# Two-part fp32r scores in head pairs, with own opening and ending, in an attention and channel-mix block

## The chip, the cores and the metric

The kernel runs on one core of a Trainium2 chip. The metric is device time in microseconds of one execution, the median of the runs. The core's engines work side by side, each through its own program in order: TensorE (PE; its weight loads are shown as PEld), VectorE (DVE), ScalarE (ACT), GpSimd (POOL), and SyncE (SP), which here only issues transfers. They meet at semaphores.

## What is computed

Eight sequences (B = 8) of N = 1024 tokens with D = 256 channels go through an adaptive layer norm, causal attention with 16 heads of 16 channels, a gated residual, a second adaptive norm and a channel mix with a token shift, gated into the residual again. The reference, cut to what matters:

```python
mod = (silu(c) @ wmod).reshape(8, 6, 1, -1)
sa, ca, ga, sb, cb, gb = (mod[:, i] for i in range(6))
ga, gb = (sign(g) * maximum(abs(g), 0.25) for g in (ga, gb))
h = layernorm(x) * (1 + ca) + sa
q, k, v = split(h @ w_in.T)                 # 16 heads of 16
p = softmax(where(causal, -inf, q @ k.T * 16 ** -0.5))
x = x + ga * ((p @ v) @ w_out.T + b_out)
h = layernorm(x) * (1 + cb) + sb
prev = h shifted by one token, zero first
xr, xk = mu_r * h + (1 - mu_r) * prev, mu_k * h + (1 - mu_k) * prev
x = x + gb * sigmoid(xr @ W_r.T) * (square(relu(xk @ W_k.T)) @ W_v.T)
```

Everything is float32. Products are made from parts: a value is rounded to a high part, what is left is a low part, and products of parts are added up.

## The kernel before

**Tiles.** A batch is one sequence. Its 16 heads are taken in G = 4 head groups (s = 0 to 3) of four heads, and each group in STEPS = 12 steps (t). Step t of COL_STEPS takes 128 keys against a stretch of 128, 256, 384 or 512 queries: keys 0 to 511 against the first half of the queries (t = 0 to 3), then keys 0 to 1023 against the second (t = 4 to 11). Six steps are 512 wide, and two each are 384, 256 and 128; 4608 query columns per head in all.

**Scores.** `fill_stacks` builds, for every head group, operands of 96 rows: six products of bf16 parts of q and k (Q_PARTS, K_PARTS), 16 rows each, placed by 12 transfers for either half of the tokens. Scores are computed twice. `row_unit` (L1052) makes them with queries on the partitions, 128 queries against a stretch of keys, into one of three banks `row_ps`; on the diagonal it adds a causal mask by a further product (L1081). VectorE reduces each bank to a maximum (`maximum`, L871). `split_max` cuts the maxima into three bf16 parts, TensorE turns them (L1066), and SyncE puts them as three more rows into the next stack. `score_columns` (L1035, L1046) makes the scores again with keys on the partitions, the maxima already subtracted, into one of three banks `col_ps`. ScalarE takes the exponential (`exps`, L715) into `weights`, GpSimd clears the part above the diagonal (L597), and `values` (L1100) multiplies with v and a column of ones, four heads side by side in four column tiles of 32, in float32. The maxima of group s + 1 are made while group s goes through exponentials.

**Dense work.** Everything else on TensorE shares the one bank `dense_ps`: the next batch's front (`front_unit`: four transposes of normalised rows at s = 1, four projections to q and k at s = 0 and s = 2 each, four to v at s = 0) and the last batch's back (`back_unit`: five units "out", "norm", "recept", "key", "value" for each quarter of the tokens, at steps BACK_STEPS after the quarter's start). TensorE takes the bank when the one before has been emptied (`claim_dense`). Around these lie the elementwise chains on the other engines: statistics and normalising on VectorE (L900, L910), the reciprocal root on GpSimd, rounding to high parts on ScalarE, low parts on GpSimd (L609, L611, L617, L638, L659, L663), gating and residuals on VectorE and GpSimd (L968, L971, L636, L671, L673).

**Order.** Each engine's program is written out by `pipeline` and `timeline`: a "first" batch with front work only, "start", "second", five "mid" and "last", then a "drain" in which the last batch's back work is done alone, its quarters TAIL_LAG = 5 ticks apart. PER_STEP says how many maxima units a step holds, and TensorE spreads them between its other instructions. Before the first batch the weights are rounded into two parts in one piece (L693 on ScalarE, L824 on VectorE), and `gates` (L840 to L854) prepares the output gates. `reciprocals` (L949) inverts the softmax sums, which go through memory and come back spread over the partitions, and L960 applies them to the attention output (`att_n`).

## Time and profile before

| | us |
|---|---|
| median of 3 runs | 1707.06 (1705.77 to 1711.83) |
| the profiled execution, its own time | 1706.89 |
| its span, first to last instruction | 1705.1 |
| TensorE busy in the span | 1407.6 |
| VectorE busy | 1184.0 |
| ScalarE busy | 911.2 |
| GpSimd busy | 738.6 |

The profile is of one execution. Busy time is the union of an engine's instructions. The ends of matmuls are modelled, so their starts are the safer reading: the distance from one start to the next is what an instruction costs when nothing is waited for. A wait is named by the engine and tile that wait and the instruction that ended it.

### The profile page before, as it was taken

To read this page: it belongs to the slowest core of one execution; us is meant where nothing else is said; L and a number is where in the kernel's file an instruction comes from. 1 tells how busy PE (TensorE), PEld (TensorE's weight loads), DVE (VectorE), ACT (ScalarE), POOL (GpSimd) and SP (SyncE) were. 2 spreads that over 40 slices of the span, in tenths; PEclk is the share of its full clock that TensorE was granted. 3 is DMA by queue.
4 is the path that set the end of the run, shared out by engine and by line. 5 is a ranking of instruction groups with operands and counts; after the bars stand their busy time and mean duration, and the time that the engine had idled before them with its cause. 6 is when DMAs were issued, how large, how long until landed. Compare 5 with 4: busy or idle time off the path is not lost.

```text
span 1705.1 us, 28546 instructions
## 1 busy us (share of the span) xinstructions
PE 1407.6 (83%) x9913; PEld 743.8 (44%) x10024; DVE 1184.0 (69%) x2306; ACT 911.2 (53%) x1795; POOL 738.6 (43%) x878
## 2 busy tenths in 40 slices
PE   3698989788887888788897888879888888989754
PEld 2253444344543445444443445434454444444344
DVE  4767667877677776877678676777767777777232
ACT  2056555555556555555555555565655655566521
POOL 4223223444454543545344444535435543444555
PEclk9899999999999999999999999989999999999956
DMA  3211121111321122111311113211221112111200
GB/s 105 63 62 52 49 94 59 49 46 57 101 68 39 46 73 93 43 55 48 102 53 50 39 58 102 67 35 48 68 95 51 57 43 80 47 61 42 65 25 19
DMA packets 101840, 102.61 MB, mean 60 GB/s; under 512 B 21296, under 2 KB 89912, under 8 KB 101696
## 3 DMA queue, kind: packets, MB, share of 16 engines
q1 hardware_dynamic: 98176, 91.59, 16.5%
q0 software_dynamic: 2560, 8.39, 1.3%
q8 instruction: 80, 1.31, 0.3%
q10 hardware_dynamic: 960, 0.79, 0.2%
q14 instruction: 64, 0.52, 0.1%
HBM read 31.74 MB, written 8.94 MB: 24 GB/s over the span
## 4 chain that ended last, share of the span: by engine, by line
PE 49%; DVE 22%; ACT 9%; POOL 7%; issue 7%; SPq 3%; DMA 2%; another core or an unknown queue 1%; POOLq 0%; DVEq 0%; ACTq 0%
PE row_ps L1076 9%; PE col_ps L1046 9%; PE val_ps L1100 8%; DVE max_a L871 8%; PE dense_ps L1110 7%; PE dense_ps L1112 5%; PE dense_ps L1111 5%; ACT weights L715 4%; PE row_ps L1081 2%; SPq L459 2%; DVE xn_c L910 2%; DVE mixed L984 2%; PE dense_ps L1129 1%; DVE max_b L871 1%
## 5 line engine op out<-in xcount | busy, mean ns | idle before, releaser
L715 ACT ACTIVATE weights<-col_ps 128x512 f32<-128x512 f32 (+1 forms) x1216 | 621.7, 580 | 461.1 <-PE col_ps L1046 342.2
L871 DVE TENSOR_REDUCE max_a<-row_ps 128x1 f32<-128x512 f32 (+3 forms) x864 | 550.0, 663 | 229.2 <-PE row_ps L1081 143.8
L1076 PE MATMUL row_ps<-k_stack,q_stack 125*128 125x512 bf16 (+3 forms) x1536 | 460.6, 338 | 58.7 <-DVE max_a L871 36.1
L1046 PE MATMUL col_ps<-q_stack,k_stack 128*128 128x512 bf16 (+3 forms) x1425 | 362.5, 328 | 52.4 <-ACT weights L715 39.9
L597 POOL TENSOR_SCALAR_AFFINE_SELECT weights<-weights 128x512 f32<-128x512 f32 x256 | 169.7, 663 | 526.2 <-ACT weights L715 520.7
L1100 PE MATMUL val_ps<-weights,v_ones 128*32 128x512 f32 (+3 forms) x3072 | 331.7, 504 | 18.1 <-POOL weights L597 16.5
L1076 PEld LDWEIGHTS row_ps<-k_stack,q_stack 125*128 125x128 bf16 x1536 | 144.7, 98 | 354.4 <-DVE max_a L871 173.3
L871 DVE TENSOR_REDUCE max_b<-row_ps 128x1 f32<-128x384 f32 (+3 forms) x352 | 213.0, 635 | 107.1 <-PE row_ps L1081 106.7
L1046 PEld LDWEIGHTS col_ps<-q_stack,k_stack 128*128 128x128 bf16 x1536 | 132.3, 98 | 202.7 <-ACT weights L715 130.8
L1081 PE MATMUL row_ps<-causal,ident_bf 128*128 128x128 bf16 x1024 | 203.1, 223 | 0.0
L1100 PEld LDWEIGHTS val_ps<-weights,v_ones 128*32 128x32 f32 x3072 | 60.9, 108 | 112.3 <-issue 66.0
L1081 PEld LDWEIGHTS row_ps<-causal,ident_bf 128*128 128x128 bf16 x1024 | 102.5, 100 | 14.6
L984 DVE SCALAR_TENSOR_TENSOR mixed<-h_diff,mus,h 128x256 f32<-128x256 f32 x128 | 76.3, 655 | 20.5 <-POOL h_diff L652 20.4
L659 POOL TENSOR_TENSOR mix_lo<-mixed,mix_hi 128x512 fp32r<-128x512 f32 x64 | 81.3, 1292 | 6.8 <-ACT mix_hi L782 6.8
L652 POOL TENSOR_TENSOR h_diff<-h 128x512 f32<-128x512 f32 x32 | 33.3, 1041 | 93.0 <-ACT h L774 92.3
L1110 PE MATMUL dense_ps<-h_hi,w_hi 128*128 128x512 f32 x128 | 61.3, 479 | 7.9 <-DVE qk_rest L942 4.2
L1129 PE MATMUL dense_ps<-ident,xn_c 128*128 128x128 f32 x128 | 21.8, 296 | 52.0 <-DVE xn_c L910 50.0
L1110 PE MATMUL dense_ps<-w_hi,o_hi 128*128 128x256 f32 x128 | 40.6, 317 | 25.2 <-POOL o_lo L638 18.9
L723 ACT ACTIVATE val_out<-val_ps 128x512 f32<-128x512 f32 x64 | 38.8, 606 | 29.0 <-PE val_ps L1100 28.5
L1110 PE MATMUL dense_ps<-mix_hi,w_hi 128*128 128x256 f32 x128 | 40.4, 316 | 15.1 <-ACT h_hi L758 12.1
L736 ACT ACTIVATE v_ones<-dense_ps 128x512 f32<-128x512 f32 x32 | 20.1, 628 | 61.0 <-PE dense_ps L1112 61.0
L1112 PE MATMUL dense_ps<-h_hi,w_lo 128*128 128x512 f32 x128 | 51.5, 403 | 0.0
(128 smaller groups left out, 2254.3 us busy)
## 6 DMA issues: line engine op xcount, KB each, us to landing
q_stack<-q_part SPq DMA_DIRECT2D x384, 64.0 KB, 2.5
k_stack<-k_part SPq DMA_DIRECT2D x372, 64.0 KB, 2.5
xa<-in_x SPq DMA_DIRECT2D x8, 1024.0 KB, 7.5
att<-val_out SPq DMA_DIRECT2D x64, 128.0 KB
recips<-recip_rows SPq DMA_DIRECT2D x32, 256.0 KB
xq<-in_x SPq DMA_DIRECT2D x28, 256.0 KB, 2.9
out<-xq POOLq DMA_DIRECT2D x28, 256.0 KB, 2.6
q_stack<-max_rows SPq DMA_DIRECT2D x192, 4.0 KB
```

The lines of the kernel that those rows point to most:

```text
L597: nc.gpsimd.affine_select(out=w, in_=w, compare_op=ALU.is_ge, fill=0.0, base=0, pattern=[[0, G], [1, P]], channel_multiplier=-1).then_inc( ...
L659: nc.gpsimd.tensor_tensor(mix_lo[:, m], mixed[:, m], mix_hi[:, m].bitcast(F32), ALU.subtract).then_inc(mix_lo_done, 1)
L715: nc.scalar.activation(weights[:, t % 2, h:h + n, 0:q1 - q0], col_ps[bank][:, 0:n * (q1 - q0)].rearrange("p (h q) -> p h q", h=n), ACT.Exp ...
L871: nc.vector.reduce_max(dest, bank[:, 0:len(heads) * (k1 - k0)].rearrange("p (h k) -> p h k", h=len(heads)), AX_X).then_inc(max_done, 1)
L984: last = nc.vector.scalar_tensor_tensor(mixed[:, m, c, :], h2_diff[:, c, :], mus[:, m, c:c + 1], h2[s % 2][:, c, 0:QT], ALU.mult, ALU.add)
L1046: last = nc.tensor.matmul(col_ps[bank][:, i * (q1 - q0):(i + 1) * (q1 - q0)], k_stack[s % 2][:, h, P * j:P * (j + 1)], q_stack[s % 2][:, h ...
L1076: last = nc.tensor.matmul(bank[:, n * width:(n + 1) * width], q_stack[stack][0:MAX_AT, h, P * i:P * (i + 1)], k_stack[stack][0:MAX_AT, h, ...
L1081: last = nc.tensor.matmul(bank[:, (n + 1) * width - P:(n + 1) * width], ident_bf[:], causal[:], start=False, stop=end, skip_group_check=True)
L1100: last = nc.tensor.matmul(val_ps[32 * h:32 * h + 32, q0 - base:q1 - base], v_ones[:, j, G * s + h].rearrange("p d a -> p (d a)"), weights[ ...
L1110: nc.tensor.matmul(dst, a_hi(c), b_hi(c), start=(c == 0), stop=False)
L1111: nc.tensor.matmul(dst, a_hi(c), b_lo(c), start=False, stop=False)
L1112: last = nc.tensor.matmul(dst, a_lo(c), b_hi(c), start=False, stop=(c == KC - 1))
```

## The change

Scores are made from two fp32r parts instead of three bf16 ones, so three products of 16 rows and two rows of maxima, 64 rows per head. Two heads, one in rows 0 to 63 and one in rows 64 to 127, are issued one behind the other into different banks. Banks are two for columns and four for rows. The maxima are gathered as columns of one tile, cut in two parts by two reductions, and turned by one transpose of 128 by 128. Maxima units come in two groups a step, at its start and after the values or the second score pair. Normalising moves from VectorE to ScalarE as scale and shift, between the exponentials; GpSimd makes the shift. The full-precision h moves from ScalarE to VectorE. The attention gate is multiplied into the output weights once per batch on GpSimd, in place of a product per quarter. Two of the four projections to v move to the batch before (s = 3), and the back units lie one step later. The opening has a program of its own on every engine, which puts the four row tiles through four banks, rounds the weights in two pieces and makes the first projections; the ending starts the last batch's quarters at ticks TAIL_START, from step 8 of the last head group, each with a bank of its own, with three elementwise steps moved from GpSimd to VectorE and the residual read from `xa`. The diff, cut to its core:

```diff
+COL_BANKS, ROW_BANKS = 2, 4
...
-Q_PARTS = (0, 0, 0, 1, 1, 2)
-K_PARTS = (0, 1, 2, 0, 1, 0)
+Q_PARTS = (0, 0, 1)
+K_PARTS = (0, 1, 0)
 ROWS = len(Q_PARTS) * HD
-MROWS = 3
-MAX_AT = P - MROWS
-FILL = 2 * len(Q_PARTS) * 16
+MROWS = 2
+ROW_TILE = 64
+MAX_AT = ROW_TILE - MROWS
+FILL = 2 * 2 * len(Q_PARTS) * 16
+PLACED = 2 * MROWS * 16
+MAX_COLS = (32, 48, 64)
 
 
...
+def bank_heads(width):
+
+    return ((0, 2), (1, 3)) if width <= QT else ((0,), (1,), (2,), (3,))
+
+
+COL_HEADS = [bank_heads(q1 - q0) for q0, q1, _ in COL_STEPS]
...
-PER_STEP = [2, 3, 3, 3, 3, 4, 4, 5, 5, 4, 2, 1]
...
+PER_STEP = [4, 4, 4, 4, 5, 2, 4, 4, 2, 4, 2, 2]
...
-V_STEPS, QK_STEPS, T_STEPS = (0, 1, 2, 3), (4, 6, 7, 8), (4, 6, 8, 10)
+V_EARLY, V_STEPS, QK_STEPS, T_STEPS = (7, 9), (0, 3), (4, 5, 7, 8), (3, 5, 7, 9)
...
-BACK_STEPS = dict(zip(BACK_UNITS, (2, 5, 9, 10, 13)))
...
+BACK_STEPS = dict(zip(BACK_UNITS, (2, 6, 10, 11, 13)))
+BACK_END = 16
+
+TAIL_START = (8, 11, 15, 18)
+TAIL_TICKS = TAIL_START[-1] + BACK_END - STEPS
...
+            def place_max(stack, half):
+
+                for part in range(MROWS):
+                    for odd in range(2):
+                        row, lo = ROW_TILE * odd + MAX_AT + part, 8 * (2 * part + odd)
+                        sp.dma_start(stack[row:row + 1, half].rearrange("p g n -> p (g n)").bitcast(F32),
+                                     max_rows[half][lo:lo + 8, :].bitcast(F32)).then_inc(max_placed[half], 16)
...
+            def gate_out_weights(b):
+
+                pool.wait_ge(gates_att_in, (b + 1) * 16)
+                pool.wait_ge(ready["transposed"], b * 4 + (8 if b < B - 1 else 4))
+                wait(pool, w_out_done, b)
+                g = gates_att[:, 0:1, :].broadcast_to([P, KC, D])
+                nc.gpsimd.tensor_tensor(gated[:], w_out[:], g, ALU.mult).then_inc(w_gated, 1)
+                pool.wait_ge(w_gated, b + 1)
+                wait(pool, ready["out"], b * G)
+                hi, lo = (w[:, W_O:W_ALL].rearrange("p (k n) -> p k n", k=KC) for w in (w_hi, w_lo))
+                nc.gpsimd.tensor_copy(hi, gated[:]).then_inc(w_out_hi_done, 1)
+                pool.wait_ge(w_out_hi_done, b + 1)
+                nc.gpsimd.tensor_tensor(lo, gated[:], hi.bitcast(F32), ALU.subtract).then_inc(w_out_done, 1)
 
...
+            def normalise(src, rstd, shift, dst, shift_done, done, count):
+
+                act.wait_ge(shift_done, count)
+                for i in range(2):
+                    last = nc.scalar.activation(dst[:, i, :], src[:, i, :], ACT.Identity, bias=shift[:, i:i + 1],
+                                                scale=rstd[:, i:i + 1])
+                last.then_inc(done, 1)
...
+            def normalise_next(b, kind, s, t):
+
+                if s == 1 and fronts(kind) and attends(kind) and t in T_STEPS:
+                    k = T_STEPS.index(t)
+                    count = b * 4 + (4 + k + 1)
+                    wait(act, ready["transposed"], count - 1)
+                    normalise(xa[:, 2 * k:2 * k + 2, :], rstd_a, shift_a, xn_a, shift_a_done, xn_a_done, count)
...
+                whole = parts[:, MAX_COLS[0]:MAX_COLS[0] + 16].bitcast(F32)
                 if half:
-                    nc.vector.tensor_tensor(src, src, max_b[:], ALU.max).then_inc(max_chain, 1)
+                    spans = parts[:, MAX_COLS[1]:MAX_COLS[1] + 32].bitcast(F32)
+                    nc.vector.reduce_max(whole, spans.rearrange("p (n c) -> p c n", n=2), AX_X).then_inc(max_chain, 1)
                     chain = chain + 1
                     dve.wait_ge(max_chain, chain)
-                nc.vector.tensor_scalar(parts[:, :, 0:G], src, -1.0, None, ALU.mult).then_inc(max_chain, 1)
...
+                pairs = parts[:, 0:64].bitcast(F32).rearrange("p (n c) -> p c n", n=2)[:, 0:16, :]
+                with nc.allow_low_precision("each output is one part of two, rounded as a part"):
+                    nc.vector.tensor_reduce(parts[:, 0:16], whole.rearrange("p (c n) -> p c n", n=1), AX_X, ALU.max,
+                                            negate=True).then_inc(max_chain, 1)
+                    dve.wait_ge(max_chain, chain + 1)
+                    nc.vector.tensor_reduce(parts[:, 16:32], pairs, AX_X, ALU.add, negate=True).then_inc(max_split, 1)
...
+            def rest_of_front(b, kind, s, t):
+
+                unit = front_unit(b, kind, s, t - 1)
+                if unit and unit[0] == "transposed":
+                    _, k, count = unit
+                    mod = mod_t[:, 8 * (b + 1):8 * (b + 1) + 4]
+                    dve.wait_ge(h_hi_done, count)
+                    wait(dve, h_lo_done, count - 1)
+                    for c in range(KC):
+                        last = nc.vector.tensor_scalar(h_full[:, c, :], dense_ps[:, c, :], mod[:, 2 + c:3 + c],
+                                                       mod[:, c:c + 1], ALU.mult, ALU.add)
+                    last.then_inc(free["transposed"], 1)
                 if unit and unit[0] == "qk":
...
+                if tail and u == 2:
+
+                    dve.wait_ge(o_hi_done, q + 1)
+                    nc.vector.tensor_tensor(o_lo[:], att_n[:, :, QT * s:QT * (s + 1)], o_hi[:].bitcast(F32),
+                                            ALU.subtract).then_inc(o_lo_done, 1)
+                if tail and u == 13:
+
+                    dve.wait_ge(k_hi_done, q + 1)
+                    nc.vector.tensor_tensor(k_lo[:], k_sq[:], k_hi[:].bitcast(F32), ALU.subtract).then_inc(k_lo_done, 1)
+                if tail and u == 15:
+
+                    dve.wait_ge(scaled_done, q + 1)
+                    nc.vector.tensor_tensor(xr, xr, recept_of(b, s), ALU.add).then_inc(out_done, 1)
+                if u == 4:
...
+                pair = COL_HEADS[t][c - COL_FIRST[t]:c - COL_FIRST[t] + 2]
+                for i in range(len(pair[0])):
+                    for odd, heads in enumerate(pair):
+                        bank, ago = bank_of(COLS * s + c + odd, COLS * G, COL_BANKS)
+                        if i == 0:
+                            wait(pe, exp_done, exp_index(b, s, c + odd) + (1 - ago))
+                        rows = slice(ROW_TILE * odd, ROW_TILE * (odd + 1))
+                        last = nc.tensor.matmul(col_ps[bank][:, i * (q1 - q0):(i + 1) * (q1 - q0)],
+                                                stack_at(k_stack[s % 2], rows, heads[i], P * j, P * (j + 1)),
+                                                stack_at(q_stack[s % 2], rows, heads[i], q0, q1),
+                                                start=(i == 0), stop=(i == len(heads) - 1), skip_group_check=True)
+                        if i == len(heads) - 1:
+                            last.then_inc(cols_ready, 1)
+
...
+                for n in range(len(pair[0])):
+                    for odd, heads in enumerate(pair):
+                        if n == 0:
+                            banks[odd] = row_bank(b, s, u + odd)
+                        rows = slice(ROW_TILE * odd, ROW_TILE * odd + MAX_AT)
+                        end = n == len(heads) - 1 and not diagonal
+                        last = nc.tensor.matmul(banks[odd][:, n * width:(n + 1) * width],
+                                                stack_at(q_stack[stack], rows, heads[n], P * i, P * (i + 1)),
+                                                stack_at(k_stack[stack], rows, heads[n], k0, k1),
+                                                start=(n == 0), stop=end, skip_group_check=True)
+                        if end:
+                            last.then_inc(rows_ready, 1)
+                for n in range(len(pair[0])) if diagonal else ():
+                    for a in range(2):
+                        for odd in range(2):
+                            rows = slice(ROW_TILE * odd, ROW_TILE * (odd + 1))
+                            end = n == len(pair[0]) - 1 and a == 1
+                            last = nc.tensor.matmul(banks[odd][:, (n + 1) * width - P + ROW_TILE * a:(n + 1) * width],
+                                                    mask_ident[rows, a, :], mask_fill[rows, a, ROW_TILE * a:P],
+                                                    start=False, stop=end, skip_group_check=True)
+                            if end:
+                                last.then_inc(rows_ready, 1)
 
             def values(b, s, t):
...
+            def open_first():
+
+                pe.wait_ge(consts_done, 3)
+                for k in range(4):
+                    pe.wait_ge(xn_a_done, k + 1)
+                    transposes(row_ps[k][:].rearrange("p (c n) -> p c n", c=KC), xn_first[:, 2 * k:2 * k + 2, :]
+                               ).then_inc(ready["transposed"], 1)
+                gate_sums()
+                pe.wait_ge(w_qk_done, 1)
+                for k in range(4):
+                    pe.wait_ge(h_lo_done, 2 * (k // 2 + 1))
+                    wait(pe, free["qk"], k - 1)
+                    qk_unit(qk_banks[k % 2], 0, k).then_inc(ready["qk"], 1)
+                pe.wait_ge(w_done, 1)
+                pe.wait_ge(setup_done, 1)
+                for k in range(2):
+                    v_unit(v_banks[k], k).then_inc(ready["v"], 1)
+                pe.wait_ge(free["v"], 2)
 
             def front(unit):
...
+                dense = dense_of(b, s)
+                if b == B:
+
+                    if name == "out":
+                        pe.wait_ge(max_done, unit_index(B - 1, G - 2, MT1) + 1)
+                    else:
+                        before = BACK_UNITS[BACK_UNITS.index(name) - 1]
+                        pe.wait_ge(free[before], count)
...
+                    row_scores(b, s, early)
+                    for c in cols[:1]:
                         score_columns(b, s, t, c)
+                    if attends(kind) if t else has_late(kind, s):
+                        values(*last)
+                    dense_step = unit or any(back_unit(*item) for item in at)
+                    if dense_step:
+                        row_scores(b, s, late)
+                    for c in cols[1:]:
+                        score_columns(b, s, t, c)
+                    if not dense_step:
+                        row_scores(b, s, late)
                     if unit:
                         claim_dense()
                         front(unit)
+                    for item in at:
+                        if back_unit(*item):
+                            if item[0] < B:
+                                claim_dense()
+                            back(*item)
+                    if t == STEPS - 1 and has_rows(kind, s):
+                        turn_max(b, s, MT1)
+
...
```

## Rows read from the trace of the kernel before

**Rows 1.** The page: busy us (share of the span), instructions.

```profile
PE 1407.6 (83%) x9913; PEld 743.8 (44%) x10024; DVE 1184.0 (69%) x2306; ACT 911.2 (53%) x1795; POOL 738.6 (43%) x878
```

**Rows 2.** Stretches: us, busy us (instructions) by engine, clock, DMA share, GB/s.

```profile
59.70:84.40 24.70, 19.41 (x85) 7.31 (x87) 24.49 (x48) 0.01 (x1) 0.69 (x1) 0.76 0.32 65
...
90.40:247.90 157.50, 142.76 (x1027) 64.92 (x1040) 113.40 (x229) 95.41 (x189) 42.96 (x60) 0.97 0.15 51
...
641.60:843.20 201.60, 171.38 (x1239) 90.51 (x1251) 149.21 (x286) 113.03 (x225) 90.87 (x108) 0.98 0.19 62
...
1443.70:1614.00 170.30, 148.52 (x1085) 76.00 (x1096) 104.79 (x206) 99.73 (x198) 76.76 (x89) 0.99 0.18 56
1614.00:1705.10 91.10, 44.54 (x210) 38.97 (x208) 28.48 (x55) 19.83 (x35) 48.33 (x49) 0.63 0.06 23
```

**Rows 3.** Waits, 641.6 to 1443.7 us: us in total, times, longest us.

```profile
ACT weights L715 <- PE col_ps L1046: 181.6, 77, 5.9
PEld row_ps L1076 <- DVE max_a L871: 83.8, 115, 2.0
PEld col_ps L1046 <- ACT weights L715: 65.5, 122, 1.7
...
PE dense_ps L1129 <- DVE xn_c L910: 29.0, 16, 3.0
```

**Rows 4.** Timeline, TensorE, around 49.6 and 800 us: start us, us, instruction.

```profile
49.56 0.40 PE L1110 MATMUL dense_ps<-h_hi,w_hi 128*128 128x512 f32 x1
...
49.80 0.40 PE L1111 MATMUL dense_ps<-h_lo,w_hi 128*128 128x512 f32 x1
...
800.13 0.34 PE L1046 MATMUL col_ps<-q_stack,k_stack 128*128 128x384 bf16 x1
800.40 1.06 PE L1100 MATMUL val_ps<-weights,v_ones 128*32 128x512 f32 x8
801.40 0.34 PE L1076 MATMUL row_ps<-k_stack,q_stack 125*128 125x384 bf16 x1
...
801.92 0.28 PE L1112 MATMUL dense_ps<-w_hi,k_lo 128*128 128x256 f32 x1
802.04 0.28 PE L1110 MATMUL dense_ps<-w_hi,k_hi 128*128 128x256 f32 x1
...
803.27 0.22 PE L1081 MATMUL row_ps<-causal,ident_bf 128*128 128x128 bf16 x1
803.33 0.60 PE L1046 MATMUL col_ps<-q_stack,k_stack 128*128 128x256 bf16 x4
```

**Rows 5.** Groups by shape: times, busy us, mean ns, idle us before.

```profile
L1046 PEld LDWEIGHTS col_ps<-q_stack,k_stack 128*128 128x128 bf16 x1536 | 132.3, 98 | 202.7 <-ACT weights L715 130.8 <-issue 18.2
...
L1110 PEld LDWEIGHTS dense_ps<-w_hi,mix_hi 128*128 128x128 f32 x128 | 25.8, 201 | 15.2 <-issue 8.8 <-DVE mix_out L992 5.0 <-DVE gated L968 1.4
```

**Rows 6.** Timeline, merged: eleven VectorE maxima, six ScalarE exponentials in a row.

```profile
62.49 6.12 DVE L871 TENSOR_REDUCE max_a<-row_ps 128x4 f32<-128x512 f32 x11
...
1593.46 3.05 ACT L715 ACTIVATE weights<-col_ps 128x512 f32<-128x512 f32 x6
```

**Rows 7.** Timeline of the opening: ScalarE, then TensorE.

```profile
15.14 3.19 ACT L693 ACTIVATE w_hi<-v_ones 128x3584 fp32r<-128x3584 f32 x1 [7.32 <-DMA v_ones<-in_w_v_t]
...
59.68 0.29 PE L1076 MATMUL row_ps<-k_stack,q_stack 125*128 125x128 bf16 x1 [6.18 <-DMA k_stack<-k_part]
```

**Rows 8.** Timeline of the ending: TensorE, VectorE, GpSimd.

```profile
1609.99 0.43 PE L1100 MATMUL val_ps<-weights,v_ones 128*32 128x128 f32 x8 [2.34 <-POOL weights L597]
...
1619.30 0.52 DVE L949 RECIPROCAL sums<-sums 128x64 f32<-128x64 f32 x1
...
1626.80 1.67 DVE L960 TENSOR_TENSOR att_n<-att,recips 128x1024 f32<-128x1024 f32 x1 [5.33 <-DMA recips<-recip_rows]
...
1665.06 0.55 PE L1110 MATMUL dense_ps<-w_hi,o_hi 128*128 128x256 f32 x1 [5.38 <-POOL o_lo L638]
...
1701.01 0.75 POOL L675 DMA_DIRECT2D out<-weights  x1 [0.30 <-POOL weights L673]
```

798 lines of the change are left out of this document (422 added, 376 removed).

## The prediction

> **What bounds the kernel now.** I read the page first, for the engines' shares [rows 1], then cut the span into its stretches [rows 2], and then asked, for the middle stretches, who waits for whom [rows 3]. No engine is full: TensorE is busy 83% of the span, VectorE 69%, ScalarE 53%. The reader is to see three parts of the span [rows 2]. The opening lasts until the first value product at 90.4 us. Then come eight batches: 157.5 us for the first, which has no back work beside it, (1443.7 - 247.9) / 6 = 199.3 us on average for each of the six that follow (the row of 201.6 is one of them), and 170.3 for the last. The ending is 91.1 us with nothing left to overlap.
>
> Inside a batch TensorE is busy 171 of 201.6 us, but those ends are modelled, so I count starts. One head group (a quarter of a batch, twelve steps) streams 4 x 4608 = 18432 columns of scores for the exponentials and as many for the maxima. Starts lie 0.11 us apart at 256 columns [rows 4] (four of them in 0.60, less about 0.27 for the last one's own time), which is one column a cycle at 2.4 GHz: 7.7 us each. The 32 mask products at 0.06 (803.27 to 803.33) make 1.9. Values take 1.00 us at 512 columns from their first start to the next instruction, against 0.85 for the columns (four passes of 512) [rows 4]; over twelve steps 10.7. Dense work of a batch is 8 x 6 x 0.23 (512 columns) + 20 x 12 x 0.12 (256) [rows 4] + 8 x 0.45 for the norms' transposes (estimated at four loads of 0.11 each) = 43 us, so 10.7 per group. With 0.9 for turning the maxima this is 39.6 per group, 158 us per batch of 199.3. The other 41 us are waits. They are spread: for ScalarE to empty a column bank, for VectorE to empty a row bank, and for the second norm's transposes, 29.0 us in 16 waits over four batches, so 7 us per batch [rows 3]. ScalarE waits for TensorE, 181.6 us in the same 802 us, so it is not the bound. TensorE in program order, fed in turn by three buffers a side, sets the step.
>
> **The change on TensorE, per head group.** Scores become three products of 16 rows plus two rows of maxima, in 64 rows, so two heads stand in the array at a time, in tiles of 64 rows.
> - Columns for exponentials and for maxima: half the stream if the two tiles run together, -3.8 and -3.8. The trace has no row tile. The nearest rows are the value products, four column tiles whose eight instructions end 1.06 us after the first starts [rows 4], where one after another the columns alone would need 3.4; so tiles can overlap here. The bounds are -3.8 and 0 each; I take -3.8, because these rows show four tiles at full overlap.
> - Operands go from bf16 to fp32r. Its matmuls keep one column a cycle: 0.12 us at 256 columns [rows 4]. Its weight load reads 201 ns against 98 [rows 5], but comes every 0.12 us under the dense products. If the two tiles' loads queue, a pair costs two such pitches, about 0.22 us, whatever its width: 48 pairs, 10.6 us for both kinds against the 7.7 taken. Bounds 0 to +2.9; I take 0 for widths of 512 and leave the rest in the range.
> - Mask: 32 pairs of half-height products for 32 whole ones: 0.3 less. Maxima turned as two fp32r tiles for eight bf16 transposes: 0.3 less.
> - Every change of tiling costs: the value product starts 0.27 us after a 384-column score whose columns take 0.16, and leaves 0.05 to 0.15 behind it [rows 4]; 0.1 a change. Score to value and back is there already. New is the change between scores and dense work, in 36 of 48 steps, twice, and twice for each turning of maxima: 22 changes per group, +2.2. No row shows such a change with row tiles: bounds 0 to +4.4, and I take the middle, as the value product is the nearest row.
>
> Sum: -7.6 - 0.6 + 2.2 = -6.0 us per group, -24 per batch. TensorE's own 158 becomes 134.
>
> The Trainium skill speaks against this edit at one point. "TensorE: Matmul & The Clock Gate", section on fast weight load, says that the fast load is not given to FP32 inputs and that a load takes its columns at 1.2 GHz, 107 ns for 128. The trace agrees in the ratio (98 against 201 ns [rows 5]). By that page alone with loads queued the sum would be -3.1 instead of -6.0; with its statement in Part 3 that loads overlap other row groups it stays -6.0.
>
> **The other engines, per batch.** VectorE, 149 busy now [rows 2]: normalising goes (16 operations of 256 columns, estimated at no more than the 0.6 of a maximum [rows 6] each: -9); gating of the attention output is folded into the weights (four 512-wide operations, estimated at the 0.6 of a maximum each: -2.5); of nine short operations on the maxima per group four go, each followed by a wait for its own end (estimated -6); the full-precision h moves here from ScalarE (8 x 0.4 = +3.3). Two short units more add 0.3 a group (+1). About 136. ScalarE, 113 [rows 2]: 16 operations of 256 columns come and 8 go, none over the 0.5 of an exponential: 117. GpSimd, 91 [rows 2]: two operations per projection go, small shift operations and three on the gated weights come; it stays far from a bound. No queue becomes the bound: SyncE issues 12 stack transfers per half as before and 4 rows of maxima for 3, and it starts key stacks one wait earlier, which takes away the few waits for them.
>
> **From work to batch.** If the waits of 41 us stay, a batch is 199.3 - 24 = 175. Norm now has a step more after its statistics and the wait for its transposes should go, -7. Against it stand the column banks, two where there were three: the second pair of a step can only be streamed when exponentials of the first pair are done. A pair of 512-wide heads keeps ScalarE some 1.0 us (six exponentials in 3.05 [rows 6]), and TensorE has values or rows to put between. I count half a microsecond for every third of 20 pairs per group, 3.3 per group at most, and take +7 per batch of a bound 0 to +13. So 175, of a range 160 to 190.
>
> **The ends.** Opening: now the weights' rounding (3.19 us for all) waits until 15.1, four row tiles pass one after another through statistics, GpSimd, transposes, ScalarE and back, and the first score starts at 59.7 after projections, parts and transfers; VectorE is busy with the gates until 62.5 [rows 6], and 24.7 us of maxima follow [rows 2, 7]. After the change statistics and turns are pipelined through four banks, projections use two, the gates are taken between parts. I estimate the first score at 36, bounds 32 to 45, and leave the 24.7 us, which VectorE's 40 reductions at 0.56 set [rows 6]. First value product at 66 (62 to 75), against 90.4. Ending: the last value product starts at 1610.0; the reciprocals come only at 1619.3, at the fifth tick of VectorE's program, and reach att_n at 1626.8; then quarters wait for each other, since all share one dense bank and GpSimd: the last one's first product starts at 1665.1 [rows 8]. After the change half the quarters start in the last twelve steps, each quarter has a bank of its own, the reciprocals go three ticks earlier (-5), and three GpSimd operations a quarter move to VectorE or before. What stays is one chain: 12 us to the normalised values, 27 for a quarter's five products with splits between (1665.1 to 1701 is 36, with the sharing), 6 for the quarter behind it, 3 to store: 50 (44 to 62), against 91.1.
>
> **Sum.** 66 + first batch 133 (157.5 - 24, no norm to gain) + 6 x 175 + last batch 149 (170.3 - 24 + 3 for tail work) + 50 = 1448; with 1.8 us around the span (1706.89 - 1705.1) 1450. The profiled run is 0.2 us below the median of 1707.06, so nothing is to be corrected.
>
> **Rivals.**
> 1. Loads of the two tiles queue (+11.5 per batch), or the two column banks cost their bound: 1450 + 8 x 11.5 = 1542. For it: fp32r loads of 201 ns. Against it: the value products' eight loads, which don't hold back their 1.06 us.
> 2. The change does not do what it says: row tiles run one after another. The score gain of 7.6 per group is gone, 30 per batch: 1450 + 8 x 30 = 1690, of which all that is left is the two ends. The trace shows only column tiles, so it can't exclude this.
> 3. Slower: TensorE stands at the second column bank. Both tiles of a pair are issued in order, and the odd head's bank is freed one exponential (0.48 us, from 3.05 for six) after the even one's. If TensorE arrives early each time, it loses that for each of 20 pairs: 9.6 per group, 38 per batch, 1450 + 8 x 38 = 1754. The ends give 65 us, so it turns into a loss from (1707 - 1450) / 8 = 32 us per batch, that is 0.4 us at every pair. Against it: ScalarE waits for TensorE now rather than the reverse, and values, rows and dense work lie between pairs.
> 4. Better: the 41 us of waits shrink with the work, and the transposes' wait goes: 160 per batch, 1450 - 8 x 13 = 1346.
>
> **How the numbers follow.** My forecast (1400 to 1500) has 0.47, rival 1 (1500 to 1580) 0.21, rival 4 (below 1400) 0.15, rival 2 (1580 to 1700) 0.11, rival 3 0.06. The range of 8 in 10 is 1360 to 1580: it takes in the forecast, rival 1 and most of rival 4, and leaves out rivals 2 and 3 and what lies below 1360. A run of this kernel can tell about 0.5%, 8.5 us. Faster by more than that: 0.47 + 0.21 + 0.15, and 0.07 of rival 2, is 0.90; the same, out of rivals 2 and 3, 0.04; slower 0.06.
>
> **What would show it.** The score pairs' second matmul starting within 0.02 us of the first, and a 512-wide pair passing in 0.22 us, shows the main term; 0.43 shows rival 2. Pairs of 128 columns at 0.22 apart show queued loads. Waits of TensorE's score products for ScalarE of some 0.5 us, twenty per group, show rival 3. A batch should last 175 us, VectorE be busy some 136 of it, the first value product start near 66 and the last one end 50 before the end. What would make the prediction wrong is above all the waits: 41 us of 199 that I let stand because no row says how two banks and fuller reordering share them. The granted clock, 0.97 to 0.99 in the batches (2.4 GHz) [rows 2], must stay there with TensorE less busy; it was 0.63 in the ending, where TensorE was busy half the time.

## The result, and the profile after

The changed kernel takes 1581.45 us (median of 4 runs, 1577.35 to 1588.32), the kernel before 1706.41 beside it: a ratio of 0.9267 (0.9227 to 0.9307), faster by 7.3%. The forecast was 1450 us, faster by 15%; the time lies just above its range of 1360 to 1580. The profiled execution of the changed kernel took 1580.16 us with a span of 1578.3.

The page's busy line of the changed kernel answers [rows 1]:

```profile
PE 1389.9 (88%) x10856; PEld 798.2 (51%) x10856; DVE 1058.8 (67%) x2155; ACT 961.5 (61%) x1916; POOL 661.9 (42%) x874
```

VectorE is shorter by 125 us, ScalarE longer by 50, as meant. TensorE, whose scores were to take half their time, is busy for only 18 us less. The stretches of the changed kernel, cut at the first value product of each batch, answer [rows 2]. Columns: stretch, its length, busy us of PE, PEld, DVE, ACT, POOL, granted clock, DMA share, GB/s.

```profile
36.00:76.20 40.20, 30.50 (x166) 19.36 (x166) 28.16 (x58) 4.44 (x9) 0.65 (x1) 0.54 0.35 64
76.20:239.40 163.20, 149.61 (x1148) 74.32 (x1146) 110.94 (x223) 98.94 (x197) 34.88 (x55) 0.91 0.22 56
...
602.80:786.60 183.80, 167.06 (x1358) 95.44 (x1358) 128.61 (x265) 119.74 (x241) 83.81 (x112) 0.96 0.26 68
...
1332.90:1507.90 175.00, 157.54 (x1132) 83.62 (x1130) 94.96 (x191) 105.15 (x211) 74.80 (x92) 0.87 0.18 48
1507.90:1578.30 70.40, 35.80 (x217) 33.32 (x216) 24.63 (x49) 25.44 (x47) 34.08 (x42) 0.76 0.09 31
```

| stretch, us | before | forecast | after | forecast missed by |
|---|---|---|---|---|
| to the first value product | 90.4 | 66 | 76.2 | +10 |
| first batch | 157.5 | 133 | 163.2 | +30 |
| six middle batches | 199.3 each | 175 each | 182.3 each | +44 |
| last batch | 170.3 | 149 | 175.0 | +26 |
| ending | 91.1 | 50 | 70.4 | +20 |

All of the gain is in the middle batches (102 us) and the two ends (35 us); the first and the last batch are longer than before. The clock is the first thing to see: before, it was 0.97 to 0.99 in all eight batches [rows 2], now it is 0.91 in the first and 0.87 in the last. Cut into pieces of 5 us, most of the loss in the last batch lies in its last head group: pieces between 1475 and 1500 us stand at 0.50, which is 1.2 GHz, with TensorE's records covering 82 to 91% of them. Before it fell, TensorE had waited 2.40 us for GpSimd's clearing (0.16 us busy in 1472 to 1474); it is back at 1.00, 2.4 GHz, from 1504, behind 5.00 us busy in 1500 to 1505. There the last batch has no maxima to make and hardly any dense work; before, the same place held 1.00 until 1608.

The waits of the middle stretch (421.4 to 1332.9 us, five batches) answer [rows 3]. Columns: who waits for whom, us in total, times, longest. The last row, set apart, is of the kernel before (641.6 to 1443.7 us, four batches).

```profile
ACT weights L804 <- PE col_ps L1219: 195.2, 249, 3.5
DVE max_parts L1026 <- PE row_ps L1267: 189.2, 164, 3.2
PEld row_ps L1256 <- DVE max_parts L1026: 98.0, 157, 1.1
...
PEld col_ps L1219 <- ACT weights L804: 68.8, 127, 1.7
...
PEld val_ps L1288 <- POOL weights L656: 42.4, 70, 1.5
...
PE dense_ps L1317 <- ACT xn_c L848: 8.3, 15, 0.6
```

```profile
PEld val_ps L1100 <- POOL weights L597: 12.6, 15, 2.3
```

ScalarE and VectorE both wait for TensorE, and TensorE for both in many pieces of half a microsecond. Its wait for the second norm has gone, from 7 to 1.7 us a batch [rows 3]; its weight loads wait 14 us a batch for column banks (16 before) and 20 for row banks (25 before: the 83.8 us of [rows 3] and 16.7 for `max_b`, over four batches). One wait has grown: the loads for the values stand 8.5 us a batch for GpSimd's clearing of the part above the diagonal, where it was 3.2. These sums can overlap with waits of the matmuls themselves, so they are not added up.

TensorE's timeline around 802 us answers [rows 4]:

```profile
802.22 0.40 PE L1300 MATMUL dense_ps<-h_hi,w_lo 128*128 128x512 f32 x1
802.55 0.50 PE L1256 MATMUL row_ps<-k_stack,q_stack 62*128 62x512 f32 x2
802.88 0.40 PE L1219 MATMUL col_ps<-q_stack,k_stack 64*128 64x512 f32 x2
803.22 1.06 PE L1288 MATMUL val_ps<-weights,v_ones 128*32 128x512 f32 x8
804.21 0.73 PE L1219 MATMUL col_ps<-q_stack,k_stack 64*128 64x512 f32 x2
804.88 0.50 PE L1298 MATMUL dense_ps<-h_hi,w_hi 128*128 128x512 f32 x1
```

Two heads of 512 columns pass as one pair, so the row tiles do run together: rival 2 is out. But a pair whose columns take 0.213 us holds TensorE for 0.33 (802.55 to 802.88, 802.88 to 803.22). In the median a 512-wide pair takes 0.34 to another pair, 0.41 to values and 0.43 to dense work; before, a 512-wide bf16 product ahead of values took 0.31 to 0.32. The dense product ahead of a pair takes 0.33 where it takes 0.23 ahead of another dense one. These pitches are where the stream's gain went, and the first runs were made to price them.

### The profile page after: what moved, and what is told of

Read it like the earlier page. It is cut to its first block, busy times and chain, and to the rows that moved or that the text cites. A ratio compares the mean times of both kernels' runs of the same rounds, so it can differ in the third digit from the quotient of the medians.

```text
span 1578.3 us, 30222 instructions
## 1 busy us (share of the span) xinstructions
PE 1389.9 (88%) x10856; PEld 798.2 (51%) x10856; DVE 1058.8 (67%) x2155; ACT 961.5 (61%) x1916; POOL 661.9 (42%) x874
## 4 chain that ended last, share of the span: by engine, by line
PE 52%; POOL 12%; DVE 12%; issue 7%; SPq 7%; ACT 6%; DMA 4%; ACTq 0%; POOLq 0%; DVEq 0%
PE val_ps L1288 13%; PE col_ps L1219 11%; PE row_ps L1256 8%; PE dense_ps L1298 6%; SPq L494 6%; DVE max_parts L1026 6%; PE dense_ps L1299 4%; PE dense_ps L1300 4%; ACT weights L804 4%; POOL weights L656 3%; DMA xq<-in_x 2%; PE row_ps L1267 2%; POOL mix_out L733 2%; POOL xq L736 2%; DVE mixed L1120 1%
## 5 line engine op out<-in xcount | busy, mean ns | idle before, releaser
L1026 DVE TENSOR_REDUCE max_parts<-row_ps 128x1 f32<-128x512 f32 (+3 forms) x1280 | 748.9, 630 | 387.1 <-PE row_ps L1267 296.4
L804 ACT ACTIVATE weights<-col_ps 128x512 f32<-128x512 f32 (+2 forms) x1280 | 643.5, 556 | 373.0 <-PE col_ps L1219 366.5
L1219 PE MATMUL col_ps<-q_stack,k_stack 64*128 64x512 f32 (+3 forms) x1536 | 388.8, 424 | 16.3 <-ACT weights L804 14.7
L1256 PE MATMUL row_ps<-k_stack,q_stack 62*128 62x512 f32 (+3 forms) x1536 | 349.5, 431 | 27.8 <-DVE max_parts L1026 18.5
L1219 PEld LDWEIGHTS col_ps<-q_stack,k_stack 64*128 64x128 f32 x1536 | 197.4, 194 | 173.4 <-ACT weights L804 135.6
L1256 PEld LDWEIGHTS row_ps<-k_stack,q_stack 62*128 62x128 f32 x1536 | 167.8, 194 | 230.4 <-DVE max_parts L1026 150.8
L1267 PE MATMUL row_ps<-mask_fill,mask_ident 64*128 64x128 bf16 (+1 forms) x2048 | 134.2, 213 | 0.0
L1267 PEld LDWEIGHTS row_ps<-mask_fill,mask_ident 64*128 64x128 bf16 x2048 | 71.6, 99 | 30.3 <-issue 15.3
L1120 DVE SCALAR_TENSOR_TENSOR mixed<-h_diff,mus,h 128x256 f32<-128x256 f32 x128 | 62.9, 551 | 19.6 <-POOL h_diff L714 19.6
L874 ACT ACTIVATE mix_out<-dense_ps 128x512 f32<-128x512 f32 x28 | 16.7, 598 | 55.3 <-PE dense_ps L1300 55.3
L1299 PE MATMUL dense_ps<-h_lo,w_hi 128*128 128x512 f32 x124 | 50.3, 405 | 0.0
L725 POOL TENSOR_TENSOR k_lo<-k_sq,k_hi 128x512 fp32r<-128x512 f32 x28 | 39.1, 1395 | 20.4 <-ACT k_hi L901 19.9
```

The costliest lines, as they stand in the source:

```text
L804: nc.scalar.activation(weights[:, t % 2, heads[0]:heads[-1] + 1:2, 0:q1 - q0], col_ps[bank][:, 0:n * (q1 - q0)].rearrange("p (h q) -> p h ...
L1026: nc.vector.reduce_max(dest, bank[:, 0:len(heads) * (k1 - k0)].rearrange("p (h k) -> p h k", h=len(heads)), AX_X).then_inc(max_done, 1)
L1219: last = nc.tensor.matmul(col_ps[bank][:, i * (q1 - q0):(i + 1) * (q1 - q0)], stack_at(k_stack[s % 2], rows, heads[i], P * j, P * (j + 1)) ...
L1256: last = nc.tensor.matmul(banks[odd][:, n * width:(n + 1) * width], stack_at(q_stack[stack], rows, heads[n], P * i, P * (i + 1)), stack_at ...
L1267: last = nc.tensor.matmul(banks[odd][:, (n + 1) * width - P + ROW_TILE * a:(n + 1) * width], mask_ident[rows, a, :], mask_fill[rows, a, RO ...
L1299: nc.tensor.matmul(dst, a_hi(c), b_lo(c), start=False, stop=False)
```

## Experiments

All are compared with the kernel before, in runs on the same chip. Its median moved from 1707.8 to 1699.0 us between the rounds of experiments, so the ratios compare more closely than the times. Where a batch is given, it is that of the one profiled execution, which was the shortest of its four in runs 8 and 9, the shortest of ten in run 10, and the longest in runs 3, 7 and 12.

**Run 1: what a pair and a change of tiling cost by themselves.** A kernel of matmuls on constant data, with no other work and nothing waited for; it computes nothing of the reference.

```diff
+for i in range(REPS):                 # full product, then a pair of 64-row tiles
+    nc.tensor.matmul(banks[4][:], w(wr, i), mr[:], start=True, stop=True)
+    nc.tensor.matmul(banks[0][:], w(wr, i)[top], mr[top], start=True, stop=True)
+    nc.tensor.matmul(banks[3][:], w(wr, i)[low], mr[low], start=True, stop=True)
```

> This kernel leaves the whole computation out: it streams rows of matmuls of one kind each on constant data, 24 of a kind, with a weight load each, and stores zeros. Theory L (a pair of row tiles pays for its fp32r weight load): full-height bf16 starts 0.22, 0.11, 0.06 us apart at 512, 256, 128 columns, full-height fp32r 0.23, 0.12, 0.11, but row-tile pairs of fp32r 0.33, 0.22, 0.16 from pair to pair, and row-tile pairs of bf16 0.22, 0.11, 0.06. Theory R (it is the row tile, not the type, that exposes the load): bf16 pairs are longer than full-height bf16 as well, by 0.03 to 0.11. My forecast had assumed 0.22, 0.12, 0.11 for fp32r pairs. A change between full height and row tiles should cost 0.1 more than the streams.

Its timeline: pairs one behind another in fp32r (L69, L70), then the alternation of a full product with a pair in fp32r (L91 to L93) and in bf16 (L95 to L97).

```profile
43.95 0.39 PE L69 MATMUL bank<-m_fp32r,w_fp32r 64*128 64x512 f32 x1
43.97 0.39 PE L70 MATMUL bank<-m_fp32r,w_fp32r 64*128 64x512 f32 x1
44.18 0.39 PE L69 MATMUL bank<-m_fp32r,w_fp32r 64*128 64x512 f32 x1
...
80.40 0.50 PE L91 MATMUL bank<-m_fp32r,w_fp32r 128*128 128x512 f32 x1
80.84 0.50 PE L92 MATMUL bank<-m_fp32r,w_fp32r 64*128 64x512 f32 x1
80.84 0.50 PE L93 MATMUL bank<-m_fp32r,w_fp32r 64*128 64x512 f32 x1
81.27 0.50 PE L91 MATMUL bank<-m_fp32r,w_fp32r 128*128 128x512 f32 x1
...
97.23 0.39 PE L95 MATMUL bank<-m_bf,w_bf 128*128 128x512 bf16 x1
97.55 0.39 PE L96 MATMUL bank<-m_bf,w_bf 64*128 64x512 bf16 x1
97.55 0.39 PE L97 MATMUL bank<-m_bf,w_bf 64*128 64x512 bf16 x1
97.87 0.39 PE L95 MATMUL bank<-m_bf,w_bf 128*128 128x512 bf16 x1
```

A pair follows a pair after 0.227 us (median of 24), as a full product follows a full one: the loads of 0.184 are hidden, those of two tiles too. At 256 columns it is 0.120, at 128 columns 0.111, in bf16 0.216, 0.109 and 0.056. So rival 1 (queued loads) is out at every width: it wanted pairs of 128 columns 0.22 us apart, and they pass in the 0.111 of one full product. Theory L of the expectation (0.33 from pair to pair) falls with it. In the alternation a round takes 0.867 us in fp32r for two times 0.227, and 0.644 in bf16 for two times 0.216. A change of tiling costs 0.206 us in fp32r and 0.106 in bf16, double the 0.1 expected for fp32r. The loads themselves last 0.183 and 0.093 there, so the cost goes with the load's length: behind a change the load isn't hidden. This is one execution, at a granted clock of 1.00 in all these rows. Part 3 of the Trainium skill's "TensorE: Matmul & The Clock Gate" says under "The mechanism" that loads overlap running products only where the row groups differ (it begins by also letting a load for the background weight buffer run ahead). By the measurement that "only" is too narrow: full products use all rows and hide theirs (0.227).

**Runs 2 to 4: a third column bank, less TensorE, less VectorE.** Run 2 takes the banks as 3 and 3. Run 3 streams 256 of the 512 columns in every 512-wide score product, run 4 lets the maxima read 256 of 512; both leave part of the scores out.

```diff
-COL_BANKS, ROW_BANKS = 2, 4                                                  # run 2
+COL_BANKS, ROW_BANKS = 3, 3
...
+                        cut = HALF // 2 if q1 - q0 == HALF else 0            # run 3, also for row products
-                        last = nc.tensor.matmul(col_ps[bank][:, i * (q1 - q0):(i + 1) * (q1 - q0)],
+                        last = nc.tensor.matmul(col_ps[bank][:, i * (q1 - q0):(i + 1) * (q1 - q0) - cut],
...
-                nc.vector.reduce_max(dest, bank[:, 0:len(heads) * (k1 - k0)].rearrange(         # run 4
+                nc.vector.reduce_max(dest, bank[:, 0:len(heads) * (k1 - k0) - cut].rearrange(
```

> Three column banks and three row banks, where the changed kernel has two and four. Theory B (TensorE stands at the second column bank, rival 3 in small): some 7 us per batch come back, 1581 becomes 1525 to 1550. Theory L (weight loads of the pairs fill TensorE's time): within 10 us of 1581, or slower by up to 30 if the fourth row bank is what VectorE needs.

Measured: 1619.68 us, ratio 0.9458 (0.9409 to 0.9506), middle batches 185.7 to 188.0 at clocks of 0.92 to 0.95. Theory B falls, and the loss is larger than theory L allowed. A third column bank, taken from the maxima, loses 38 us, 3 to 6 of them in every middle batch. The trace shows both sides of the exchange (440.3 to 1376.3 us): the loads' waits for column banks fell from 14 to 9 us a batch, those for row banks rose from 20 to 26.

> Every 512-wide score product streams only 256 of its columns; everything else reads as much as before (half of these scores are left over from earlier, so the output is not the reference's). TensorE has 24 pairs x 0.107 us less per head group, 10.2 per batch, VectorE and ScalarE the same. If TensorE's stream sets the step: 8 to 10 us per batch, 65 to 80 in all, about 1505 to 1515. If VectorE, ScalarE or a chain of short waits sets it: less than 30 in all.

Measured: 1581.4 us, ratio 0.925 (0.9207 to 0.9293), the case of less than 30 us: no gain from 10 us a batch less on TensorE (96 pairs of 512 columns, each shorter by 0.106). Middle batches are longer than in the changed kernel, 183.4 to 187.9, at a clock of 0.88 to 0.92 where it was 0.96 to 0.98. What is taken from the stream is met by a lower clock. That the clock took the gain is argued from the price that run 8 puts on it; no run shortened the products and held the clock up.

> VectorE reduces only 256 of the 512 columns of a one-head bank (the maxima are then not over all keys, so the output is not the reference's); TensorE and ScalarE have the same work. 24 reductions per group lose some 0.25 us each, 24 us per batch of VectorE's 129. If TensorE sets the step: no more than 25 us in all, above 1555. If VectorE sets it: 100 or more, below 1480.

Measured: 1563.3 us, ratio 0.9134 (0.9092 to 0.9175), for 24 us a batch less on VectorE: middle batches 177.5 to 183.9. VectorE is no bound by its work.

**Run 5: less ScalarE.** The 512-wide exponentials take 256 columns (the rest of the weights stays zero).

```diff
-                nc.scalar.activation(weights[:, t % 2, heads[0]:heads[-1] + 1:2, 0:q1 - q0],
+                nc.scalar.activation(weights[:, t % 2, heads[0]:heads[-1] + 1:2, 0:q1 - q0 - cut],
```

> Of every 512-wide exponential ScalarE takes only the first 256 columns (the other 256 of the weights stay as they were at the start, so the output isn't the reference's); 240 x 0.22 us per batch estimated, some 50 of its 120 us, go. With the maxima halved 24 us of VectorE's went and the middle batch stayed at 177 to 182 us, and with the score products halved it stayed at 184 to 188. Theory A (TensorE in program order, with its changes of tiling, sets the step, and the third engine is no different from VectorE): middle batches stay at 178 to 183, the time at 1550 to 1580. Theory B (the column side is the bound: product, two exponentials, clearing, values, with only two banks): middle batches fall by 15 or more, to 165 or less, the time to 1470 or less.

Measured: 1544.51 us, ratio 0.9068 (0.9003 to 0.9133). ScalarE fell from 120 to 100 us a batch, by 20 and not by 50 as I had estimated; middle batches are 175.9 to 181.3, 179.1 in the mean where the changed kernel has 182.3. Theory A holds on batches; its time was missed by 5 us on the good side.

**Run 6: the same score products in bf16.** Only the type changes: the upper halves of the same stacks are read (coarser scores).

```diff
-                return stack[rows, half, head // 2, n0 - HALF * half:n1 - HALF * half]
+                return stack[:].bitcast(BF16)[rows, half, head // 2, 2 * lo + 1:2 * hi:2]
```

> The score products read the upper halves of the same stacks as bf16 (so scores are coarser and the output differs). Columns, tiles, banks and order stay; only the type changes. In the stand-alone run a change of tiling cost 0.106 us with bf16 operands and 0.206 with fp32r. Theory A (each first pair after a change pays its load, TensorE sets the step): some 88 changes per batch end on a score pair, half as much again lie inside groups that wait, so 9 to 12 us a batch go: middle batches 171 to 174, the time about 1500 to 1515, unless the clock falls. Theory C (loads are hidden in the kernel): pitch of pair to next pair stays at 0.33 us and the batches at 182.

TensorE's timeline of this run: dense product, maxima pair, score pair, values.

```profile
787.96 0.40 PE L1301 MATMUL dense_ps<-h_hi,w_lo 128*128 128x512 f32 x1
788.28 0.40 PE L1257 MATMUL row_ps<-k_stack,q_stack 62*128 62x512 bf16 x2
788.52 0.33 PE L1220 MATMUL col_ps<-q_stack,k_stack 64*128 64x384 bf16 x2
788.79 1.06 PE L1289 MATMUL val_ps<-weights,v_ones 128*32 128x512 f32 x8
```

The 512-wide pair passes to the next in 0.24 us where it took 0.33: the load is 0.1 us of each such pitch, in the kernel as in run 1, and theory C falls. Counted as described in the next section, TensorE's own work falls by 9 us a batch. The time is 1533.82 us, ratio 0.9006 (0.8942 to 0.907). Middle batches are 174.9 to 180.8 long, 178.0 in the mean, so only about half of the 9 us reached them; the first batch fell from 163.2 to 150.8. Theory A's place was right, its 171 to 174 and its 1500 to 1515 were not.

**Run 7: two queues' order.** ScalarE's copies of v ahead of the second half's stack issues; SyncE spreads the reciprocals ahead of the load of the mix gate.

```diff
-                        load_mix_gate(b)
                         spread_recips(b - 1, 1)
+                        load_mix_gate(b)
...
+                    if half:
+                        act.wait_ge(ones_done, 1)
+                        for k in range(2):
+                            act.wait_ge(ready["v"], k + 1)
+                            nc.scalar.activation(v_ones[:, 2 * k:2 * k + 2, :, :, 0],
...
                     act.wait_ge(free["qk"], 2 * (half + 1))
                     for r, part in enumerate(K_PARTS):
```

> Two changes of order alone, in stretches that don't touch. Opening: ScalarE copies the two v tiles ahead of its six issues for the second half of the stacks. Ending: SyncE spreads the reciprocals before it loads the mix gate, for which it waits. Theory (both waits are a queue's own order): first score at 37.5 in place of 43.2 us, first value product 4 to 6 us earlier; from the last value product to the end 64 in place of 70 us; time 1568 to 1572. Rival (something else arrives just as late: stack transfers of the second half, or VectorE's gates until 36.9): first value product unchanged within 1 us; the ending the same 70 us, because the mix gate is then what is late.

First the opening of the changed kernel (ScalarE, its queue of issues, then TensorE):

```profile
29.83 5.56 ACTq L784 DMA_DIRECT2D k_stack<-k_part  x6
...
35.44 0.60 ACT L777 ACTIVATE q_part<-dense_ps 128x512 fp32r<-128x512 f32 x1 [6.46 <-issue]
...
38.11 3.79 ACTq L784 DMA_DIRECT2D k_stack<-k_part  x6
42.01 0.62 ACT L790 ACTIVATE v_ones<-col_ps 128x512 f32<-128x512 f32 x1 [5.48 <-issue]
...
43.18 0.69 PE L1256 MATMUL row_ps<-k_stack,q_stack 62*128 62x128 f32 x4 [7.49 <-ACT v_ones L790]
```

Six issues hold ScalarE for 5.6 and again for 3.8 us, and TensorE waits 7.49 us for copies that could be made before. Then the ending, SyncE and VectorE, of the changed kernel, and below it of run 7:

```profile
1518.06 0.32 SPq L547 DMA_DIRECT2D gates_mix<-gate_rows  x1
1518.49 0.36 SPq L518 DMA_DIRECT2D recip_rows<-sums  x1
...
1526.76 1.23 DVE L1135 TENSOR_TENSOR att_n<-att,recips 128x1024 f32<-128x1024 f32 x1 [7.70 <-DMA recips<-recip_rows]
```

```profile
1519.83 0.32 SPq L518 DMA_DIRECT2D recip_rows<-sums  x1
...
1525.30 0.32 SPq L547 DMA_DIRECT2D gates_mix<-gate_rows  x1
1526.49 2.23 DVE L1136 TENSOR_TENSOR att_n<-att,recips 128x1024 f32<-128x1024 f32 x1 [0.20 <-DMA recips<-recip_rows]
```

With the last value products at 1507.9 and 1515.1, `att_n` comes 18.9 us behind them in the changed kernel and 11.4 in run 7. The first score starts at 38.1 (43.2), the first value product at 71.1 (76.2), the ending lasts 66.8 (70.4). Both places were named rightly, the ending's gain is 3.6 and not 6. The whole, 1577.69 us, ratio 0.9257 (0.9192 to 0.9323), missed its 1568 to 1572 and can't be told from the changed kernel: its middle batches lasted 181.1 to 187.9 at clocks of 0.94 to 0.98, and gave the 9 us back.

**Run 8: products that nobody reads.** They fill TensorE's pauses in the first maxima, the first batch and the last head group.

```diff
+                    extra = 0
+                    if kind == "first" and has_rows(kind, s):
+                        extra = 2
+                    if kind == "start" and s > 0 and not dense_step and t % 2 == 0:
+                        extra = 2
+                    if kind == "last" and s == G - 1:
+                        extra = 4
...
+                        for i in range(extra):
+                            nc.tensor.matmul(dense_flat, w_hi[0:ROW_TILE, 0:P], w_hi[0:ROW_TILE, 0:HALF], start=True,
```

> Products whose result nobody reads (64 rows, 512 columns, 0.23 us each at 2.4 GHz) are added on TensorE into the free dense bank: two per step in the first maxima, two in every other step without dense work in the first batch from the second head group on, four per step in the last batch's last head group. Some 24 + 30 + 48 of them, 23 us of work. Theory D (the granted clock, 0.54 in the opening, 0.91 in the first batch, 0.87 in the last, is lost because TensorE stands still too often): the clock rises to 0.95 or more in these stretches and each becomes shorter: first batch 163 to 157, last batch 175 to 168, time 1565. Rival (the fillers take more from the path than the clock gives back): each stretch becomes longer by up to the fillers' own time, 1585 to 1600.

Stretches of run 8: two middle batches, in which its program is that of the changed kernel, and the last batch with its 48 fillers.

```profile
242.00:421.30 179.30, 161.82 (x1341) 93.11 (x1341) 127.82 (x264) 118.87 (x240) 79.26 (x107) 0.99 0.26 68
962.80:1146.80 184.00, 168.10 (x1352) 96.06 (x1352) 128.73 (x265) 119.55 (x241) 83.73 (x111) 0.95 0.25 68
1330.40:1495.80 165.40, 152.91 (x1180) 85.92 (x1178) 95.03 (x191) 105.02 (x211) 74.85 (x92) 0.99 0.18 51
```

The last batch, with more work on TensorE, is 9.6 us shorter at a clock of 0.99 in place of 0.87: theory D holds there. (Run 7, whose last batch has the changed kernel's program and no fillers, took 172.5 us for it at 0.89, so the gain is 7 to 10.) It fails in the opening, where the clock stayed at 0.50 and the fillers cost 2 us, and in the first batch (0.94, 163.8 us). The middle batches give the clock's price by themselves: one program, one execution, 178.2 to 179.4 us at 0.99 to 1.00 and 183.6 to 184.0 at 0.95. Run 7, with the same program there, has 186.0 to 187.9 at 0.94 to 0.95. Nothing was changed between these batches, so they show that length and clock go together; only the last batch's fillers changed the clock by an edit. In all 1576.88 us (1567.83 to 1585.27), ratio 0.9257 (0.9184 to 0.933), 12 us above what was expected.

**Runs 9 and 10: fewer changes of tiling.** In run 9 dense work follows the values directly, in run 10 the values come behind both score pairs, directly ahead of dense work. Either has three changes in a step with dense work, not four.

```diff
                         values(*last)                     # run 9
-                    if dense_step:
-                        row_scores(b, s, late)
-                    for c in cols[1:]:
-                        score_columns(b, s, t, c)
-                    if not dense_step:
-                        row_scores(b, s, late)
                     if unit:
                         claim_dense()
                         front(unit)
...
+                    for c in cols[1:]:
+                        score_columns(b, s, t, c)
+                    row_scores(b, s, late)
...
-                    if attends(kind) if t else has_late(kind, s):        # run 10
-                        values(*last)
                     dense_step = unit or any(back_unit(*item) for item in at)
...
+                    if attends(kind) if t else has_late(kind, s):
+                        values(*last)
                     if unit:
```

> In each step the dense product follows the values at once, and only then come the late maxima pair and the second score pair. A step with dense work then changes its tiling three times and not four; over a batch some 30 changes go, each 0.2 us by the trace of the changed kernel (a 512-wide pair ahead of values or dense work takes 0.40 to 0.43 us, its columns 0.213). Theory A (the changes of tiling, mis-sized in the forecast, are what keeps TensorE's own work where it was, and TensorE sets the step): 6 us a batch, time 1535 to 1550. Rival (the order is worth more than the changes: rows that come late let VectorE stand, dense work that comes early waits for its operands): no gain or a loss, 1580 to 1640.

Its timeline, TensorE and ScalarE:

```profile
923.68 0.64 PE L1288 MATMUL val_ps<-weights,v_ones 128*32 128x256 f32 x8
...
926.25 0.39 PE L1298 MATMUL dense_ps<-w_hi,h_hi 128*128 128x256 f32 x1 [1.93 <-DVE xq L1104]
```

Measured: 1859.79 us, ratio 1.0928 (1.0883 to 1.0972), far beyond the rival's 1640. TensorE stands 1.93 us for VectorE to empty the dense bank, with the second score pair of the step queued behind; middle batches take 219.6 to 225.2 us. In the changed order the second pair and the late maxima cover this wait.

> The other way to the same number of changes: values go behind both score pairs, directly ahead of the dense product. Theory A: the same 6 us a batch less as with the dense product moved. Rival (the second pair waits longer for its column bank, since nothing of TensorE's lies between the two pairs but, at times, a maxima pair): slower than the changed kernel, by 0.3 to 0.5 us for each of 48 steps, 15 to 24 us a batch, time 1700 to 1770.

```profile
PEld col_ps L1219 <- ACT weights L804: 136.8, 238, 1.4
...
PE col_ps L1219 <- ACT weights L804: 66.3, 117, 0.8
```

These are its waits over 750 us. Measured: 1690.69 us, ratio 0.9937 (0.9903 to 0.9971), middle batches 193.4 to 197.3. With nothing between the two pairs of a step TensorE stands at the second column bank, 117 times over that stretch for 0.57 us on average: this is rival 3 of the forecast, at the size of its 0.48 us, made by taking the values away from between the pairs. The cost was 11 to 15 us a batch, below the rival's 15 to 24.

**Run 11: both orders and fillers, also ahead of the transposes.** Four a step in the last head group, three full products ahead of each transposing unit.

```diff
+                    if kind == "last" and s == G - 1:
+                        fill(4, ROW_TILE)
...
+                        if unit[0] == "transposed":
+                            fill(3, P)
```

> The two changes of order, and products that nobody reads where the trace shows TensorE's clock granted at 0.5: four a step in the last batch's last head group (there the clock went from 0.87 to 0.99 and the batch from 175 to 165.4 us with them), and three full ones (0.23 us each) ahead of each of the four transposes in every second head group, where TensorE waits for normalised rows and the clock falls behind it. Theory D (a middle batch at a clock of 1.00 lasts 178 us and at 0.95 184): middle batches at 0.99 to 1.00 and 177 to 179 us, first value product at 71, ending 66, time 1540 to 1550. Rival (the clock falls at another place as often, or the fillers stand ahead of work that was ready): middle batches stay at 181 to 186 and the time at 1560 to 1575.

Measured: 1568.81 us, ratio 0.9215 (0.9173 to 0.9257). First value product 72.0, last batch 164.3 at a clock of 1.00, ending 66.8, as expected. The middle batches took 180.8 to 184.7 at 0.96 to 0.98: the rival holds there, and the filler ahead of the transposes is useless.

**Run 12: VectorE and ScalarE shortened together** (the cuts of runs 4 and 5).

> Both the 512-wide maxima and the 512-wide exponentials take only 256 columns (the output isn't the reference's); VectorE has some 104 us and ScalarE some 100 us of work in a batch, TensorE all of its own. With either alone the middle batch was 176 to 184 us. Theory A (TensorE in program order is the bound; what it still waits for are the two others by turns, so only both together show it): a middle batch comes down to TensorE's own work, some 150 to 156 us by the pitches, plus a few us: 158 to 168, time 1430 to 1490, if the clock stays above 0.95. Theory E (fixed distances between the engines, semaphores and starts, hold the step, not their work): 172 to 180, time 1530 to 1560.

```profile
579.00:759.50 180.50, 164.00 (x1355) 94.07 (x1353) 105.25 (x265) 99.93 (x241) 83.44 (x111) 0.94 0.26 69
```

Measured: 1526.83 us, ratio 0.8975 (0.8929 to 0.9022), middle batches 174.5 to 180.5 (178.2 in the mean) at clocks of 0.94 to 0.97. Both engines now have 75 us and more to spare in a batch, and TensorE still waits for a row bank 16.5 us a batch (66.2 in four batches; 19.6 before the cuts). Theory A falls as it was put; the batches lie where theory E put them (the time is 3 us below its range). But one partner was left as it was: the loads for the values now wait 11.5 us a batch for GpSimd's clearing, where it was 8.5. Whether a shorter clearing would let the batch follow no run tried.

**Run 13: maxima products in bf16, with both orders and the last head group's fillers.** A maximum only shifts the exponent, so its products may be coarse. Run 6's edit is applied to the products into `row_ps` alone.

> The two changes of order and the fillers of the last head group, and the maxima products (whose result only shifts the exponent and cancels in the quotient) read the upper halves of the stacks as bf16; the score products of the exponentials stay fp32r. With all score products in bf16 the load ahead of a pair fell by 0.1 us and middle batches by 4 to 5. Theory A: half of the changes of tiling end on a maxima pair, so 2 to 3 us a batch: middle batches 176 to 181, first value product 70, last batch 163, ending 67: time 1535 to 1550. Rival (the mixed types add a change of their own between a maxima pair and a score pair): middle batches stay at 181 to 186, time 1560 to 1570.

Measured: 1545.1 us, ratio 0.9104 (0.9049 to 0.9159), the best of the versions that keep fp32r for the exponentials' scores and leave nothing out, 2.3% below the changed kernel's median and 1.8% by the two ratios. Middle batches took 180.1 to 181.9 at a clock of 0.95 to 0.97, about 3 us less than the 184 that run 8 shows at 0.95; the first batch took 155.3, the last 165.4. The time was within theory A's range, the batches at its upper end and, in two of six, just above it.

## Why the prediction was wrong

The direction was right and the size was not. The time lies in rival 2's band (1580 to 1700), but that rival's mechanism is out, as is the queueing of rival 1. By its own steps:

**Streams: right.** TensorE's own work in a middle batch is a count of mine and not a measurement, made from starts: each instruction at the short pitch of its kind ahead of its neighbour. Streams are 136 us before and 105 after, so 31 less, where the forecast had 30.4 and 2.4 for masks and turns. Row tiles run in pairs, fp32r costs 11 ns a pair.

**Changes of tiling: the term that was mis-sized.** What stands beside the streams rose from 19 to 39 us a batch, +20 where the sum had +8.8. The count was near (forecast 88 new changes a batch; the trace has 168 against 96, so 72 new: 48 from a pair to values, 40 from values to a pair, 8 from values to dense work, 32 from a pair to dense work, 40 back). The price was not: 0.2 us (run 1: 0.206), of which 0.1 is the fp32r load, which no longer hides (run 6 takes it away: 0.33 to 0.24). And the old changes to and from values became dearer by that load as well, which the sum did not have at all. "Loads 0", and with it the 0.1 a change that was read from bf16 rows, was the failed step: I had read them as hidden because they are hidden where like follows like. TensorE's own work went from 155 to 144 us by this count, where the forecast had 158 to 134: 11 us and not 24. The total hangs on which pitch of a kind is called short. Other choices, from the least to the lowest quarter, give 151 to 153 before and 129 to 150 after, so the 11 may be off by some 10. Without such a choice, 168 changes at run 1's 0.206 less 96 at the forecast's 0.1 make +25 a batch, again far above +8.8.

**Waits: a second error, of the other sign.** The batch of 182 us holds 38 of waits, at a full clock (178.2, run 8) 34, where 41 and no change was taken. So the middle batch was missed by only 3 us at a full clock, as the sum of +10 and -7. The norm's wait went as forecast. The +7 for two column banks does not show: the loads' waits for them are 14 us a batch and were 16, and a third bank took 5 off and gave 6 back at the row banks (run 2). Rival 3's mechanism is real (run 10); with the values between the pairs it did not make these waits longer than before. Rival 4 was partly right. This second error hid part of the first: without the 7 us a batch the time would have been some 40 us further above the range, and that it lies only 1.5 us above is luck. What the 34 us consist of is shown only in part. They are hand-overs: of banks, and of the weights that GpSimd clears, which the forecast did not count. Cutting the partners' work took only 2 to 4 us off the mean of the middle batches (180.7, 179.1 and 178.2 in runs 4, 5 and 12, of 182.3), while changing the order of issue added 12 to 40 (194.8 and 222.0 in runs 10 and 9).

**The clock: a condition that broke.** The forecast ended on "must stay there"; it did not, and nothing in the sum had a price for it. In middle batches 0.95 in place of 1.00 goes with 5 us (run 8; with 8 in run 7), so by the smaller price the 0.96 to 0.98 of the changed kernel cost 2 to 4 each, some 20 in six. In the last batch 0.87 cost 7 to 10 (runs 7 and 8). In the batches at the two sides TensorE's own work by the same count fell by 12 and 15 us and not by 24, which is 12 of the first batch's miss of 30 and 9 of the last one's 26; the clock is worth up to 9.6 of the last one's, and by the middle batches' price some 10 of the first one's. What is left, 8 and 7 us, I can't assign. Run 3 shows the trap: 10 us a batch less to stream, a clock of 0.88 to 0.92, and no gain. Together, of the 130 us missed the changes of tiling account for some 80, the clock for 40 and the two ends for 30; the waits gave 40 back, and 20 stay open.

**Opening and ending.** The first score was expected at 36 and came at 43.2: ScalarE's twelve stack issues (5.6 and 3.8 us) stood ahead of the copies of v; I had counted transfers on SyncE and none on ScalarE. Run 7 took 5.1 of it back. From there to the first value product it is 33.0 us where 30 were forecast. In the ending the forecast had 12 us to the normalised values; they came after 18.9, because SyncE held the reciprocals behind a load that waits for another quarter's end, the queue that the sum passed over (run 7: 11.4). The other miss is the distance between quarters: the last split of a quarter comes at 1541.1, 1550.3, 1560.4 and 1570.1, so about 9.7 us apart where I had put 6 for the one behind.

**Other engines: right.** VectorE has 128.6 us in a batch (forecast 136), ScalarE 119.7 (117), neither a bound.

## What to carry to other kernels

Where products of different tilings alternate, count the changes and price each with the whole load that it exposes (0.21 us in fp32r, 0.11 in bf16 here), the old ones as well, for a load read as hidden is hidden only where like follows like. Before taking work from TensorE, look up which stretches will no longer keep it busy: the granted clock may take the gain back, and useless products can pay (175 to 165 us in one batch) or not (opening, transposes). A score product that only yields a shift may be coarser than the one that yields the result (bf16 in run 13), and issuing transfers costs the engine that does it time ahead of everything behind them (0.6 to 0.9 us each on ScalarE here).

## What the runs showed of the hardware

Fp32r pairs in two row tiles follow each other every 227, 120 and 111 ns at 512, 256 and 128 columns, bf16 pairs every 216, 109 and 56. Changing between full products and pairs costs 0.206 us in fp32r and 0.106 in bf16 (run 1). One program showed 178.2 and 184.0 us for equal batches within one execution, at clocks of 1.00 and 0.95, with nothing in its order that differs.

In the opening one small operation of VectorE took 3.05 us and its like behind it 0.40. The timeline of the changed kernel, GpSimd and VectorE:

```profile
29.68 3.52 POOL L638 MEMSET v_ones<- 128x4096 f32 x1
...
30.43 3.05 DVE L992 TENSOR_SCALAR mixed<-xn_c 8x512 f32<-8x512 f32 x1
...
33.41 0.40 DVE L993 TENSOR_SCALAR mixed<-xn_c 8x512 f32<-8x512 f32 x1
```

It ended at 33.48, 0.28 us behind GpSimd's clearing (29.68 and 3.52). The kernel before has the clearing at another place, and the delay went with it:

```profile
54.77 0.40 DVE L840 TENSOR_SCALAR mixed<-xn_c 8x512 f32<-8x512 f32 x1
...
56.88 3.51 POOL L583 MEMSET v_ones<- 128x4096 f32 x1
...
57.52 3.15 DVE L845 TENSOR_SCALAR mixed<-mixed 8x512 f32<-8x512 f32 x1
```

There the operation that took 3.05 us (L840, L992) takes 0.40, and one that takes 0.41 in the changed kernel (L845, L997) takes 3.15 and ends at 60.67, again 0.28 behind the clearing. So it is the clearing that holds these operations up. Not every operation is held: the copy from PSUM at 29.73, inside the clearing, took 0.67 us, as it did in the kernel before with GpSimd idle. The Trainium skill, "SBUF — State Buffer", section "SBUF: two separate sides", states that VectorE shares one of its pairs of ports with GpSimd as an exclusive lock, so that an operation of VectorE that uses both pairs waits for the whole of a GpSimd operation that began first. The rows agree in time; that it is this lock no row shows.
